# Spreading the output gates over all partitions by a transfer from memory instead of by matrix products

## The reference, cut to what matters

```
mod = (silu(c) @ wmod).reshape(16, 6, 1, 128)
sa, ca, ga, sb, cb, gb = mod[:, 0], ..., mod[:, 5]
ga = (2 * (ga >= 0) - 1) * maximum(abs(ga), 0.25)
gb = (2 * (gb >= 0) - 1) * maximum(abs(gb), 0.25)
h = layernorm(x) * (1 + ca) + sa
x = x + ga * attention(h)
h = layernorm(x) * (1 + cb) + sb
x = x + gb * (max_prob * expert(h))
```

## Time and profile before

| | us |
|---|---|
| median of three runs | 534.43 |
| lowest, highest | 531.08, 536.52 |
| the profiled execution | 533.16 |
| its span, first to last instruction | 531.4 |
| TensorE busy | 387.3 |
| DVE busy | 424.9 |
| ScalarE busy | 273.7 |
| GpSimd busy | 270.4 |
| mean granted clock of TensorE | 0.856 |

### The profile page before, as it was taken

One profiled execution on the slowest core, in us unless ns is written; L12 is line 12 of the kernel. 1 busy time (PEld: TensorE's weight loads), 2 busy tenths in 40 slices (PEclk: granted clock), 3 DMA queues, 4 the chain that ended last, 5 costly groups with the idle time before them and its releaser, 6 DMA issues.

```text
span 531.4 us, 8977 instructions
## 1 busy us (share of the span) xinstructions
PE 387.3 (73%) x2675; PEld 352.1 (66%) x2675; DVE 424.9 (80%) x1218; ACT 273.7 (51%) x592; POOL 270.4 (51%) x315
## 2 busy tenths in 40 slices
PE   2938460878949669766196966678999899999980
PEld 1313120878949669756196866668989898999980
DVE  5849999999899996999999899965885641549733
ACT  2777764966125324545555546272554554664620
POOL 1134223959999958642838837501221576232330
PEclk9987885887788779977587977798999996999996
DMA  8347679970000000930310001114310113223105
GB/s 210 60 69 113 80 98 154 132 42 1 1 0 2 1 0 10 379 89 0 56 25 2 0 1 35 52 29 87 71 36 27 36 56 99 76 78 106 50 31 163
DMA packets 50031, 33.98 MB, mean 64 GB/s; under 512 B 10960, under 2 KB 46560, under 8 KB 49984
## 3 DMA queue, kind: packets, MB, share of 16 engines
q1 hardware_dynamic: 46976, 28.01, 28.0%
q0 software_dynamic: 3008, 5.40, 3.3%
HBM read 14.21 MB, written 10.26 MB: 46 GB/s over the span
## 4 chain that ended last, share of the span: by engine, by line
DVE 46%; PE 35%; issue 8%; ACT 3%; DMA 3%; POOL 3%; SPq 1%; POOLq 0%; DVEq 0%; ACTq 0%
PE bank L702 11%; PE bank L717 6%; DVE U L1458 5%; DVE S L1471 5%; PE bank L561 5%; DVE p L1465 4%; DVE p L1452 4%; PE bank L541 4%; DVE big L1407 4%; DVE X L1409 3%; PE bank L545 2%; DVE big L1392 2%; POOL placed_y L902 1%; PE bank L574 1%; DVE XN L1288 1%
## 5 line engine op out<-in xcount | busy, mean ns | idle before, releaser
L541 PE MATMUL bank<-prod_o,ID 128*128 128x128 f32 x512 | 81.9, 326 | 42.1 <-POOL prod_o L285 19.0
L541 PEld LDWEIGHTS bank<-prod_o,ID 128*128 128x128 f32 x512 | 76.5, 236 | 43.5 <-POOL prod_o L285 19.6
L902 POOL DMA_INDIRECT placed_y<-Q,place x46 | 44.2, 960 | 108.2 <-DVE Q L1675 69.7
L702 PE MATMUL bank<-Q,p 128*128 128x128 f32 x736 | 97.5, 282 | 0.0
L702 PEld LDWEIGHTS bank<-Q,p 128*128 128x128 f32 x736 | 92.5, 198 | 0.1
L1038 ACT ACTIVATE p<-S,GAM 128x64 f32<-128x64 f32 x126 | 48.0, 410 | 74.1 <-DVE S L1471 73.2
L278 POOL TENSOR_TENSOR prod_o<-Q,ST 128x1024 f32<-128x1024 f32 x28 | 61.9, 2211 | 40.6 <-PE bank L545 32.4
L1199 ACT ACTIVATE p<-big 128x1024 f32 x46 | 48.5, 1056 | 46.1 <-PE bank L702 43.4
L1471 DVE TENSOR_REDUCE S<-p 128x64 f32<-128x320 f32 x126 | 55.2, 472 | 5.0 <-ACT p L1038 5.0
L1458 DVE TENSOR_REDUCE U<-p 128x32 f32<-128x288 f32 x128 | 52.5, 438 | 0.0
L1452 DVE TENSOR_TENSOR p<-S,bank 128x256 f32<-128x256 f32 x128 | 49.1, 406 | 0.7 <-ACT bank L1033 0.7
(11 more groups left out here) (228 smaller groups left out, 801.0 us busy)
## 6 DMA issues: line engine op xcount, KB each, us to landing
big<-in_L_ffn_w_dram SPq DMA_DIRECT2D x1, 4096.0 KB, 13.5
big<-big SPq DMA_DIRECT2D x16, 192.0 KB, 5.3
Q<-sorted_h SPq DMA_DIRECT2D x46, 64.5 KB, 1.9
sorted_h<-ZERO SPq DMA_DIRECT2D x2, 1472.0 KB, 17.3
X<-in_L_attn_x_dram SPq DMA_DIRECT2D x8, 256.0 KB, 4.5
big<-big SPq DMA_DIRECT2D x16, 128.0 KB, 4.6
X<-Q SPq DMA_DIRECT2D x32, 64.0 KB, 2.5
K<-placed_y SPq DMA_DIRECT2D x8, 256.0 KB, 3.3
```

The source lines that it names most:

```text
L541: pe.matmul(ps, ID[:, :], prod_o[:, k % 2, i, :], start=(i == 0), stop=False, skip_group_check=True)
L702: m = pe.matmul(bank[(1, 6)[g % 2] + k][:, c * P:(c + 1) * P], W1E[g % 2][:, f:f + P], XST[:, g % 3, :], start=True, stop=True)
L902: pool.indirect_dma_start(placed_y[g // NF], bass.IndirectOffsetOnAxis(ap=place[:, g:g + 1], axis=0), YS[:, g % YR, :], None).then_inc(sem ...
```

## The change

The gates go to memory once (`gate_h`, 8 KB), behind the moves of slice 1's keys, queries and values, and come back by one transfer that reads the same 8 KB for each of the 128 partitions. SP issues it in the loop of the expert stage behind load 21, after waiting for the store and for the last reader of WOG. The products on TensorE and the evacuations on ScalarE are gone. DVE waits for the transfer ahead of `finish(0, 0)`.

```diff
@@ (tensors in memory)
+    gate_h = nc.dram_tensor("gate_h", (B * D,), F32, kind="Internal").ap()
@@ (SP, behind the moves of slice 1)
+            sp.wait_ge(sem("gate_ready"), 1)
+            sp.dma_start(gate_h.rearrange("(b d) -> b d", b=B), GATE[:, 1, :]).then_inc(sem("gates_out"), 16)
             sp.wait_ge(sem("const_set"), 1)
@@ (SP, the loop of the loads)
                 sp.dma_start(XS[:, g % XR, :], sorted_h[s][j * P:(j + 1) * P, :]).then_inc(sem(f"xs_in{g % XR}"), 16)
                 if g in (MOVE - 1, MOVE):
                     move_outputs(sp, 1, [g - MOVE + 1])
+                if g == NF - 2:
+                    sp.wait_ge(sem("gates_out"), 16)
+                    sp.wait_ge(sem("att_ps", 1), 4)
+                    sp.dma_start(GB[:, :, :].rearrange("p b d -> p (b d)"),
+                                 gate_h.rearrange("(a x) -> a x", a=1).broadcast_to([P, B * D])).then_inc(sem("gb_in"), 16)
@@ (TensorE)
-            def gate_rows(q):
-
-                if q == 0:
-                    pe.wait_ge(sem("h2_evac"), 8)
-                elif q == 1:
-                    pe.wait_ge(sem("pos_ready"), 2)
-                else:
-                    pe.wait_ge(sem("gb_evac"), q - 1)
-                for i in range(4):
-                    b = 4 * q + i
-                    m = pe.matmul(bank[(5, 4)[q % 2]][:, i * P:(i + 1) * P], ID[0:B, b:b + 1].broadcast_to([B, P]), GATE[:, 1, :], start=True, stop=True)
-                m.then_inc(sem("gb_ps"), 1)
@@ (TensorE, g == NF)
                     for k in (2, 1):
                         second(g - k)
-                    for q in range(4):
-                        gate_rows(q)
                     for k in range(2):
                         turn_x(g + k)
@@ (ScalarE)
-            def gate_evac(q):
-                act.wait_ge(sem("gb_ps"), q + 1)
-                act.activation(GB[:, 4 * q:4 * q + 4, :], bank[(5, 4)[q % 2]][:, :].rearrange("p (n d) -> p n d", n=4), ACT.Copy)\
-                    .then_inc(sem("gb_evac"), 1)
-
@@ (ScalarE, g == NF - 1)
-                    for q in range(4):
-                        gate_evac(q)
                     exponentials(1)
@@ (DVE, finish)
+                if s == 0 and q == 0:
+                    dve.wait_ge(sem("gb_in"), 16)
                 dve.wait_ge(sem(f"y_in{q}"), 16 * (s + 1))
```

## The result

| | before | after |
|---|---|---|
| median of six runs each | 534.33 us | 526.89 us |
| lowest to highest | 531.08 to 536.52 | 525.09 to 528.10 |
| ratio, 95% interval | | 0.9882, 0.9851 to 0.9912 |
| profiled execution, its span | 533.16, 531.4 | 527.69, 525.9 |

The kernel is 7.4 us or 1.2% faster; 526.2 was forecast.

A forecast was written before the change was run, and what follows sets the result against it. No engine bounds the whole run; at the border between slices TensorE is on the chain without a break. 5.7 + 2.6 - 0.1 = 8.2 us off 533.16 gives 525.0, or 526.2 from the median shown; range 522.5 to 531.5.

The forecast's parts named there:

- (a): At the border between the expert stage's slices, removing L636's sixteen products and their evacuations from TensorE's chain gains 5.7 us.
- (b): Behind the border, TensorE's clock stays full over slice 1's first six half tiles and three turns: gain 2.6 us.
- Rival B: TensorE's clock falls anyway, in the pauses before 441 us: 4.8 us given back, 531.0 us; chance 0.14.
- Does the gain last: Behind the border all of slice 1 moves forward together; tile 23's scatter, under 1 us late, costs nothing.
- (c): The 8 KB store on SP, behind slice 1's raw moves, costs 0, at worst 0.6 us.
- (d): The 1 MB load on SP behind load 21 takes 5 us and is hidden, even at 12 us: cost 0.
- (e): DVE's wait for `gb_in`, the 1 MB load, is already met: no cost.
- C: At the border another wait, tile 23's rows or tile 25's weights, replaces L636; 3 us late gives 529.2; chance 0.10.
- D: The 1 MB load uses one transfer engine, 44 us; load 22 waits, TensorE stands 18 us: 544 us; chance 0.04.
- E: L636 at the border was hidden, so its removal moves nothing: 534 us; chance 0.02.

The follow-up runs named there:

- the three other groups: The changed kernel run again unaltered beside the kernel before, on one chip and on two others: ratios 0.9875, 0.9918 and 0.9875.

## Why the prediction was right, point by point

**(a), 5.7 us.** From the end of the last W2 product to the first products of slice 1 the chain took 6.79 us (441.17 to 447.96) and takes 0.95 (443.76 to 444.71): 5.8. Nothing else took the place of L636. All was ready: load 23 was issued at 440.07 and its rows turned at 443.6; ScalarE's exponential and both table loads were over before the first half of tile 23 (silu(23) begins at 445.70, directly behind it).

**(b), 2.6 less 0.1 us.** Six half tiles and three turns take 6.02 us (444.71 to 450.73) instead of 8.30: 2.3. The clock stayed, and the 5.7 of full clock were exceeded by 0.3, of which 0.27 is the row 448.57, 1.16 instead of 0.89: tile 25 waits for its copy of W1. I had put 0.1. The reason was right as well. In two kernels with sixteen products at the same place, the clock falls with 16 rows and not with 128; they differ beside the rows only in the moving operand. Rival B had the pauses of the border do it: they stand in the execution with 128 rows, and in all of the changed kernel's, without a fall. By the Trainium skill's account (TensorE: Matmul & The Clock Gate, Part 1), activity releases the throttle; the runs add that PE's busy share in the records isn't that activity. A window busy for 5.20 of 5.20 us had a clock of 0.71.

The sum was right, its parts were cut differently from what the runs show. The prediction put all of L636's 5.46 us down to the products and their evacuations and 2.6 to the clock. But the fall also stretched L636 itself: the half clock cost 4.7 us in all, which is what rival B's working made of 10.1 us of it (4.8), the products 3.4, and the waits for the evacuations next to nothing. The sum is the same 8.1.

**Does the gain last.** Yes: 60.03 us and 15.3 us behind the border in both. GpSimd issued the scatter of tile 22 at 451.68 and that of tile 23 right behind it, at 452.94; from tile 24 on it waits for TensorE's tiles again.

**(c), (d), (e).** The transfer took 5.4 us where 5 were taken, and landed at 410.7, 19 us ahead of the turn of the tile loaded behind it. The store took 0.58 us of SP.

**The total.** Local gain 8.1, of 8.2 forecast; the medians show 7.4, and 5.2 to 6.8 in the three other groups, all of them less. That the first comes so near to the forecast is in part luck. The profiled execution gained 5.5 only, because it came to the border 2.6 us later. The way to the border takes 441.2 to 444.1 us in the six profiled executions before the other chips; that all of the difference to 8.1 is of this kind, and nothing of it the transfers', is likely by the rows and isn't shown.

**The rivals.** B didn't come. C didn't come, and its price stays unmeasured. D doesn't hold for 128 partitions; with 127 the transfer takes the 44 us that were worked out and holds up the load behind it, and the cost to the kernel wasn't measured. E is excluded by the result.

## What to carry to other kernels

Matrix products that use few rows of the array and spread or copy data can be cheap by their count and dear by the clock that falls under them: here 3.4 us of products and 4.7 us of half clock. Look at the granted clock behind such a stretch, not at the busy share in it. A table that must stand in all partitions can come by a transfer with a repeated source, issued long before its reader, if the number of partitions lets it spread over all engines (128 did, 127 didn't); and a bank freed by such a change may be what ends the next pause.

## What the runs showed of the hardware that wasn't expected

- On two of three chips both kernels took 26 to 28 us more, most of it in one stretch of 22 us in which TensorE was busy for a quarter to two fifths of the time and DVE and ScalarE for about a tenth or less, while GpSimd issued scatters. It wasn't there on the first chip. What released them at its end isn't in the trace.
- A transfer of 127 partitions took 44 us, 24 GB/s, about a sixteenth of the best slice (379), and the next issue behind it held SP for 18.6 us. 128 partitions with the same source took 3.2 to 4.1 us.
- The 8 KB store from 16 partitions took 5.0 us to landing, nearly as long as the 1 MB.
